# Banded attention stage rewritten: unrolled query blocks, row maximum on 32 queries by 160 keys, stacking transfers from SBUF

## The chip, the cores and the metric

The program runs on one core of one Trainium2 chip. The metric is the device time of one execution in microseconds. The program is four stages in a row (attention, a routed two-level expert layer, a state-space layer, a soft mixture of experts); only the first, attention, is changed, and an all-engine barrier stands behind it.

## The reference

With x of shape 2048 x 128, 16 heads of 8 channels:

```
xn  = layernorm(x)                       # no gain, no offset
q, k, v = split(xn @ Wqkv + bqkv)        # 16 heads of 8
s   = (q . k) * 8**-0.5,  only where |i - j| <= 64, else the lowest float
out = softmax(s) @ v
x   = x + layernorm(out @ Wout + bout)
... three more stages follow, each x = x + layernorm(stage(layernorm(x)))
```

## The kernel before

**Number format.** q and k are split into three bf16 parts each (h, m, l: high, middle, low). A score is one matmul over 48 rows, six products of parts times 8 channels, held in two "stacks": `qs` and `ks`, 128 partitions, where partitions 0 to 63 hold the even heads and 64 to 127 the odd ones (48 rows of parts and, in `ks`, 16 rows of flags that forbid the padding keys). Eight head pairs `j` lie side by side along the free axis.

**Set-up.** x is loaded in one transfer, normalized (`ln_x`), transposed by TensorE, and projected chunk by chunk (512 tokens, L514 to L525). ScalarE and VectorE make the three parts (L464 to L468, L348 to L352). SyncE then writes the parts to DRAM (`parts_scratch`, L274) and reads them back into the stacks, 24 transfers of 8 partitions each per group of tokens (L283; groups of 512, 512 and 1024 tokens). Meanwhile GpSimd fills both stacks with constants (L290, L291).

**Windows.** Queries go in 17 blocks ("windows") of 128, offset by 64, each against 256 keys. VectorE first copies a window of the stacks to `kw` and `qw` (`window`, L358, L359) and of v to `vw` (`window_v`, L362). For each window and each group g of four heads (4 groups):
- `natural(w, g)`: two matmuls of 512 columns with the identity put the band mask (-1e30 outside) into PSUM (L536), four matmuls of 128 queries by 256 keys add the scores (L541). VectorE takes the negated maximum of each query over the 1024 columns (`maxima`, L366). `parts(w)` splits the 16 maxima of each query into three bf16 parts (L375 to L381), TensorE transposes them (`maxima_t`, L581) and VectorE takes them back (`m_t`, L388).
- `transposed(s, g)`: four matmuls of 256 columns with a selection matrix add the maxima (L553), eight matmuls add the scores, keys on the partitions (L559). ScalarE exponentiates 1024 columns at once (`exps`, L474). GpSimd zeroes what lies outside the band with two affine selects (L316, L318).
- `values(s, g)`: eight matmuls in column tiles of 32 multiply by v and a column of ones (L573).
Then `values_nat` transposes (L587), VectorE divides (`norm`, L398, L401), `attn_t` transposes (L592). `project` (L599) runs in the last window for all 16 tiles; bias, `ln_y` and the addition to x follow at the end (L437, L75 to L143).

**Order.** Each engine has its list written out by hand: `body` for one window, run by `steps`: window 0, a hardware loop over 14 windows, two per round, then windows 15 and 16. In one round TensorE does `natural` of window s+1 beside `transposed` of window s; the scores of `natural` have two pairs of PSUM banks, those of `transposed` one pair, so `transposed(g)` waits for the exponential of g-1. Engines are in order, and all waits are semaphores.

## Time and profile before

| | |
|---|---|
| median of 3 runs | 856.33 us (854.08 to 858.31) |
| profiled execution, its own time | 861.29 us |
| its span, first to last instruction | 859.5 us |
| busy share of the span: TensorE, VectorE, ScalarE, GpSimd | 77%, 61%, 40%, 42% |
| mean granted TensorE clock | 0.904 of full |

The profile has a page of the whole execution and a trace that can be asked for groups of instructions, for the busy time in a stretch, for waits, for transfers and for the instructions in order of time. Attention is the stretch from 0 to 291.9 us, where the first transfer of the next stage is issued.

### The profile page before, as it was taken

The page shows a single profiled execution, that of the slowest core. Times are in us where ns is not written, and L with a number is a line of the kernel's source. Part 1 is how long each engine was busy: PE and PEld are TensorE (multiplying, and loading weights), DVE is VectorE, ACT ScalarE, POOL GpSimd, SP SyncE. Part 2 cuts the span into 40 slices and gives each one's busy share as a digit, 9 for nine tenths or more (in the row PEclk, how much of TensorE's full clock was granted, in tenths as well). Part 3 has the DMA queues.
Part 4 walks back from the last instruction along what each step waited for, and adds up shares of the span by engine and source line. Part 5 has one row for each costly group of instructions (what it writes and reads, how often), then busy time and mean ns, then how long its engine had stood idle before and what let it go on. Part 6 is the DMA issues. An engine that isn't in the chain of part 4 may idle for free. (4 is left out here: it accounts for less than half of the span.)

```text
span 859.5 us, 18332 instructions
## 1 busy us (share of the span) xinstructions
PE 660.1 (77%) x7554; PEld 384.0 (45%) x7554; DVE 525.7 (61%) x1094; ACT 344.9 (40%) x522; POOL 359.2 (42%) x330
## 2 busy tenths in 40 slices
PE   0617888888888279976977498058998988999995
PEld 0302444444445179876876234023333344444442
DVE  8647667676664733342413667869999974406266
ACT  1421433444344573242414552346544536434320
POOL 9202444444444300000001253228999974966530
PEclk9967999999999559997977689669999999999998
DMA  3156552000000364000000640000000000000000
GB/s 76 37 107 108 89 72 32 0 0 0 0 0 2 111 199 100 3 4 2 4 4 5 261 112 0 0 1 0 0 1 0 0 1 1 1 0 1 12 13 25
DMA packets 17327, 29.76 MB, mean 35 GB/s; under 512 B 3248, under 2 KB 13168, under 8 KB 16240
## 3 DMA queue, kind: packets, MB, share of 16 engines
q1 hardware_dynamic: 17264, 28.87, 14.1%
q8 instruction: 46, 0.75, 0.4%
q14 instruction: 17, 0.14, 0.1%
HBM read 24.54 MB, written 4.19 MB: 33 GB/s over the span
## 5 line engine op out<-in xcount | busy, mean ns | idle before, releaser
L474 ACT ACTIVATE pr_exp<-at_psum 128x1024 f32<-128x1024 f32 x68 | 69.6, 1023 | 131.9 <-PE at_psum L559 131.9
L366 DVE TENSOR_REDUCE pr_neg_max<-at_psum 128x4 f32<-128x1024 f32 x68 | 83.2, 1225 | 49.8 <-PE at_psum L541 49.8
L316 POOL TENSOR_SCALAR_AFFINE_SELECT pr_exp<-pr_exp 128x512 f32<-128x512 f32 x68 | 47.1, 692 | 159.0 <-ACT pr_exp L474 159.0
L1493 POOL TENSOR_TENSOR all_phi_b<-all_phi_b,mo_work 128x512 f32<-128x512 f32 x56 | 71.1, 1269 | 43.3 <-ACT mo_work L1699 38.6
L749 POOL TENSOR_TENSOR all_x<-all_x,ff_x_blocks 128x512 f32<-128x512 f32 x3 | 3.8, 1263 | 173.0 <-ACT ff_x_blocks L940 173.0
L1514 PE MATMUL all_psum<-all_phi,mo_xt 128*128 128x512 f32 x128 | 67.1, 651 | 7.3 <-ACT mo_work L1681 5.6
L536 PE MATMUL at_psum<-band_mask,all_ident_bf 128*128 128x512 bf16 x136 | 43.1, 400 | 38.3 <-DVE pr_q_window L359 38.3
L1463 POOL TENSOR_TENSOR mo_work<-mo_work,mo_max 128x1024 f32<-128x1024 f32 x32 | 61.3, 1916 | 22.1 <-DVE mo_max L1755 22.1
L1547 PE MATMUL all_psum<-mo_xt,all_phi_centred 128*128 128x512 f32 x128 | 65.4, 591 | 0.0
L1600 PE MATMUL all_psum<-mo_work,mo_y_slots 128*128 128x512 f32 x128 | 62.5, 595 | 1.8 <-DVE mo_work L1803 1.8
L1699 ACT ACTIVATE mo_work<-all_psum 128x512 f32<-128x512 f32 x64 | 37.7, 601 | 60.6 <-PE all_psum L1547 60.6
L1469 POOL TENSOR_TENSOR mo_dispatch<-mo_work,mo_rsum 128x1024 f32<-128x1024 f32 x32 | 61.3, 1917 | 0.0
L1523 PE MATMUL all_psum<-mo_dispatch,mo_xn 128*128 128x512 f32 x128 | 60.2, 595 | 0.0
L1685 ACT ACTIVATE mo_work<-mo_work 128x1024 f32<-128x1024 f32 x32 | 33.9, 1058 | 55.5 <-POOL mo_work L1463 55.5
L1803 DVE TENSOR_TENSOR mo_work<-mo_work,all_psum 128x512 f32<-128x512 f32 x64 | 38.9, 683 | 11.9 <-PE all_psum L1589 11.9
L553 PE MATMUL at_psum<-pr_neg_max_t,band_select 128*128 128x256 bf16 x272 | 41.6, 276 | 5.9 <-ACT pr_exp L474 5.5
L318 POOL TENSOR_SCALAR_AFFINE_SELECT pr_exp<-pr_exp 128x512 f32<-128x512 f32 x68 | 45.8, 674 | 0.0
L1514 PEld LDWEIGHTS all_psum<-all_phi,mo_xt 128*128 128x128 f32 x128 | 23.6, 200 | 46.9 <-ACT mo_work L1681 24.0
L1755 DVE TENSOR_REDUCE mo_max<-mo_work 128x32 f32<-128x1024 f32 x32 | 38.7, 1208 | 7.1 <-ACT mo_work L1681 7.1
L573 PE MATMUL at_psum<-pr_exp,pr_v_window 128*32 128x128 f32 x1088 | 41.7, 278 | 1.4 <-POOL pr_exp L318 1.4
L1762 DVE TENSOR_REDUCE mo_sum<-mo_work 128x32 f32<-128x1024 f32 x32 | 38.7, 1209 | 0.0
L1523 PEld LDWEIGHTS all_psum<-mo_dispatch,mo_xn 128*128 128x128 f32 x128 | 24.5, 192 | 31.0 <-issue 29.9
(339 smaller groups left out, 1340.2 us busy)
## 6 DMA issues: line engine op xcount, KB each, us to landing
all_expert_w<-in_expert_w SPq DMA_DIRECT2D x1, 4096.0 KB, 18.3
ff_b_up<-in_b_up SPq DMA_DIRECT2D x1, 2048.0 KB, 10.2
ff_a_up<-in_a_up SPq DMA_DIRECT2D x1, 2048.0 KB, 16.1
ff_w_down<-in_w_down SPq DMA_DIRECT2D x2, 1024.0 KB, 20.5
at_q_stack<-parts_scratch SPq DMA_DIRECT2D x24, 64.0 KB
at_k_stack<-parts_scratch SPq DMA_DIRECT2D x24, 64.0 KB
at_q_stack<-parts_scratch SPq DMA_DIRECT2D x12, 128.0 KB
at_k_stack<-parts_scratch SPq DMA_DIRECT2D x12, 128.0 KB
```

The lines of the kernel that those rows point to most:

```text
L316: nc.gpsimd.affine_select(out=e[:, g, :, 0, :], in_=e[:, g, :, 0, :], compare_op=ALU.is_ge, fill=0.0, base=0, pattern=[[0, GH], [-1, P]], ...
L318: nc.gpsimd.affine_select(out=e[:, g, :, 1, :], in_=e[:, g, :, 1, :], compare_op=ALU.is_ge, fill=0.0, base=0, pattern=[[0, GH], [1, P]], c ...
L366: nc.vector.tensor_reduce(negm[:, GH * g:GH * g + GH].rearrange("p (u r) -> p r u", r=2), psum[:, SN + 2 * (g % 2):SN + 2 * (g % 2) + 2, : ...
L474: nc.scalar.activation(e[:, g, :, :, :].rearrange("p h j q -> p (h j q)"), psum[:, ST:ST + 2, :].rearrange("p b n -> p (b n)"), ACT.Exp).t ...
L536: nc.tensor.matmul(psum[:, SN + 2 * (g % 2) + r, :], c["identb"][:, :], c["mask"][:, :, :].rearrange("p a b -> p (a b)"), start=True, stop ...
L1463: nc.gpsimd.tensor_tensor(cells(ls[:, u % 4, :]), cells(lc[:, u % 4, :]), to_cells(mn[:, u % 4, :]), ALU.subtract).then_inc(sub_done, 1)
L1469: nc.gpsimd.tensor_tensor(cells(dn[:, u % 4, :]), cells(ls[:, u % 4, :]), to_cells(rs[:, u % 4, :]), ALU.mult).then_inc(d_ready, 1)
L1493: nc.gpsimd.tensor_tensor(tot[:, ch % 2, :], first, ec[:, ch % 2, j, :], ALU.add).then_inc(added, 1)
L1514: last = nc.tensor.matmul(psum[:, 2 * hf + k, :], xt[:, P * z:P * z + P], phi_d[:, HALF * hf + W * k:HALF * hf + W * k + W], start=True, s ...
L1523: last = nc.tensor.matmul(psum[:, 4 + 2 * hf + k, :], xn[:, z, :], dn[:, u % 4, W * k:W * k + W], start=(z == 0), stop=(z == NT - 1))
L1547: nc.tensor.matmul(psum[:, n % 3, :], phi[:, P * j:P * j + P], xt[:, cols], start=False, stop=True).then_inc(cl_done, 1)
L1600: nc.tensor.matmul(psum[:, 5 + ch % 2, :], yt[:, j, :], ec[:, ch % 2, j, :], start=(j == 0), stop=(j == NJ - 1)).then_inc(y_done, 1)
```

## The change

- The stacks are filled straight from the parts in SBUF, without DRAM: the projection's columns are laid out so that 64 contiguous partitions hold one half. There are again 24 transfers of 8 partitions per group, but ordered by part: first all that need h, then m, then l, so that the first can go before the others are computed. The input is loaded in three pieces.
- The padding keys are flagged in one row (48), set up by six transfers `rows_in`; GpSimd fills only the edges of the stacks.
- The negated maximum enters the score matmul itself: its three parts are three more rows (49 to 51) of `qs`, against ones in `ks`. They get there by two small transfers per window (`maxima_in`), for which SyncE waits; the matmuls of `transposed` now take 52 rows and no selection matmul stands before them.
- The maximum is taken over 32 queries by 160 keys (the band of 32 queries is 160 wide): a unit is two heads of one half, eight matmuls of 49 rows, 32 query columns, 160 keys, in four column tiles. No mask matmul: VectorE adds a 128x160 mask and takes the minimum in one instruction, two per unit, 16 per window.
- A unit of `transposed` is two heads too (four matmuls, one PSUM bank), and the exponential is 128x512, eight per window. Both `natural` and `transposed` have rings of three banks. No copies `kw`, `qw`, `vw`: the loop is unrolled and reads the stacks directly.
- `natural` runs two windows ahead. `project` runs one tile per window within the loop, the bias as a matmul with a row of ones; ScalarE takes the result, VectorE its statistics. The residual of tiles 0 to 11 is done in the last two windows.
- TensorE runs 24 matmuls of 512 columns (`keep_warm`) ahead of the first window.

The diff, cut to its core (`+` and `-` lines only, declarations and most waits left out):

```diff
-                            sp.dma_start(scratch["hml".index(k), :, :, r0:r1].rearrange("w p n -> p w n"), kept[:, :, r0:r1]).then_inc(bounced[ch], 16)
-                                    sp.dma_start(stack[p0:p0 + 8, :, pad + r0:pad + r1], rows[half][:, :, r0:r1]).then_inc(stacked[ch], 16)
+                def stack(group, kind):
+                    r0, r1 = STACKS[group]
+                    sp.wait_ge({"h": hi_ready, "m": mid_ready, "l": low_ready}[kind], 2 * r1 // 512)
...
+                                    sp.dma_start(dst[p0:p0 + DH, :, pad + r0:pad + r1], part[k][64 * half:64 * half + 64, which, r0:r1]).then_inc(stacked[group], 16)
+                def maxima_in(w):
+                    sp.wait_ge(mt_ready, w + 1)
+                    for half in range(2):
+                        p0 = 64 * half + PARTS
+                        sp.dma_start(qs[p0:p0 + 3, :, w * P:w * P + P], m_t[24 * half:24 * half + 24, w % 2, :]).then_inc(nm_in[w % 2], 16)
+                for kind in "hml":
+                    stack(0, kind)
+                stack(1, "h")
+                maxima_in(0)
+                stack(1, "m")
+                stack(1, "l")
+                maxima_in(1)
+                for n, kind in enumerate("hml"):
+                    stack(2, kind)
+                    maxima_in(2 + n)
+                for w in range(5, NW):
+                    maxima_in(w)
...
-                    nc.gpsimd.memset(ks[:, :, :].rearrange("p j n -> p (j n)").bitcast(F32), 0.0)
-                    nc.gpsimd.memset(qs[:, :, :].rearrange("p j n -> p (j n)").bitcast(F32), ONE_ONE).then_inc(filled, 2)
+                nc.gpsimd.memset(qs[:, :, 0:64], 0.0)
...
-                        nc.vector.tensor_copy(kw[:, wp, :, :], ks[:, :, bass.ds(w * P, 2 * P)])
-                        nc.vector.tensor_copy(qw[:, wp, :, :], qs[:, :, bass.ds(w * P, P)]).then_inc(win, 1)
-                        nc.vector.tensor_reduce(negm[:, GH * g:GH * g + GH].rearrange("p (u r) -> p r u", r=2),
+                        last = v.tensor_tensor_reduce(out=masked[:, 2 * (k % 3) + i, :], in0=psum[:, SN + n % 3, WIN * i:WIN * i + WIN], in1=mask[:, :], scale=-1.0, scalar=3.0e38,
+                                                      op0=ALU.add, op1=ALU.min, accum_out=nm[:, r, 0, j:j + 1])
...
+                    nc.scalar.activation(e[:, m // 2, 2 * (m % 2):2 * (m % 2) + 2, :, :].rearrange("p h j q -> p (h j q)"), psum[:, ST + n % 3, :], ACT.Exp, scale=scale).then_inc(exp_done, 1)
...
-                            nc.tensor.matmul(psum[:, SN + 2 * (g % 2) + r, :], c["identb"][:, :], c["mask"][:, :, :].rearrange("p a b -> p (a b)"),
+                def natural(w, m):
...
+                    for i in range(2):
+                        r, j = head(m, i)
+                        rows = slice(64 * r, 64 * r + PARTS)
+                        for q in range(0, P, QC):
+                            k0 = w * P + q
+                            last = nc.tensor.matmul(psum[q:q + QC, SN + n % 3, WIN * i:WIN * i + WIN], qs[rows, j, k0:k0 + QC], ks[rows, j, k0:k0 + WIN], start=True, stop=True)
+                def transposed(w, m):
+                    n = NU * w + m
+                    if m == 0:
+                        pe.wait_ge(nm_in[w % 2], 32 * (w // 2 + 1))
+                    if n >= 3:
+                        pe.wait_ge(exp_done, n - 2)
+                    for i in range(2):
+                        r, j = head(m, i)
+                        rows = slice(64 * r, 64 * r + PARTS + 3)
+                        for b in range(2):
+                            last = nc.tensor.matmul(psum[:, ST + n % 3, 256 * i + P * b:256 * i + P * b + P], ks[rows, j, (w + b) * P:(w + b) * P + P], qs[rows, j, w * P:w * P + P], start=True, stop=True)
+                def project(t):
...
+                    nc.tensor.matmul(psum[:, SN + n % 3, 0:P], one[:, :], bias[:, :], start=True, stop=False)
+                    nc.tensor.matmul(psum[:, SN + n % 3, 0:P], a_t[:, col:col + P], wout[:, :], start=False, stop=True).then_inc(sn_done, 1)
...
+                keep_warm(WARM)
...
+                for s in range(NW):
+                    for m in range(NU):
+                        transposed(s, m)
+                        if s + 2 < NW:
+                            natural(s + 2, m)
+                        if m == 0 and s >= 1:
+                            values(s - 1, 2)
+                        if m == 1 and s >= 1 and s + 1 < NW:
+                            maxima_t(s + 1)
+                        if m == 1 and s >= 3:
+                            project(s - 3)
+                        if m == 2 and s >= 1:
+                            values(s - 1, 3)
+                        if m == 4 and s >= 1:
+                            values_nat(s - 1)
+                        if m == 4:
+                            values(s, 0)
+                        if m == 6 and s >= 1:
+                            attn_t(s - 1)
+                        if m == 6:
+                            values(s, 1)
```

VectorE's order in one round is `maxima(s + 2, m)` for m = 0 to 7, the statistics of one projected tile behind m = 1, `norm(s - 1)` behind m = 5, and `parts(s + 2)` at the end. ScalarE's is `exps(s, m)`, with `take_maxima(s + 1)` behind m = 1, the copies of the values and of the projected tile behind m = 2, and that of the attention tile behind m = 6.

## Rows read from the trace of the kernel before

**Rows 1.** Busy time, clock and transfers in four stretches of attention and in two windows.

```profile
core 0: us, PE busy (x) PEld busy (x) DVE busy (x) ACT busy (x) POOL busy (x), PEclk, DMA share, GB/s
15.00:65.00 50.00, 16.30 (x64) 10.45 (x64) 29.86 (x45) 16.09 (x30) 11.77 (x10) 0.84 0.32 65
...
74.00:278.00 204.00, 173.02 (x2409) 93.31 (x2409) 135.44 (x253) 82.05 (x101) 89.70 (x136) 0.99 0.18 29
278.00:292.00 14.00, 3.17 (x13) 2.19 (x11) 8.79 (x34) 4.95 (x11) 3.56 (x9) 0.50 0.00 0
```

**Rows 2.** TensorE's instructions in order of time, one window in the loop.

```profile
157.49 0.60 PE L536 MATMUL at_psum<-band_mask,all_ident_bf 128*128 128x512 bf16 x2 [1.34 <-DVE pr_q_window L359]
158.03 0.39 PE L541 MATMUL at_psum<-pr_k_window,pr_q_window 64*128 64x256 bf16 x4
158.35 0.61 PE L553 MATMUL at_psum<-pr_neg_max_t,band_select 128*128 128x256 bf16 x4
158.90 0.40 PE L559 MATMUL at_psum<-pr_q_window,pr_k_window 64*128 64x128 bf16 x8
159.22 0.66 PE L573 MATMUL at_psum<-pr_exp,pr_v_window 128*32 128x128 f32 x16
159.82 0.61 PE L536 MATMUL at_psum<-band_mask,all_ident_bf 128*128 128x512 bf16 x2
...
166.94 1.12 PE L573 MATMUL at_psum<-pr_exp,pr_v_window 128*32 128x128 f32 x32
...
169.56 0.60 PE L536 MATMUL at_psum<-band_mask,all_ident_bf 128*128 128x512 bf16 x2 [1.34 <-DVE pr_q_window L359]
```

**Rows 3.** Groups by line and shape, one window (157.5 to 169.55 us).

```profile
L366 DVE TENSOR_REDUCE pr_neg_max<-at_psum 128x4 f32<-128x1024 f32 x4 | 4.9, 1225 | 3.0 <-PE at_psum L541 3.0
L474 ACT ACTIVATE pr_exp<-at_psum 128x1024 f32<-128x1024 f32 x4 | 4.1, 1024 | 6.5 <-PE at_psum L559 6.5
...
L553 PE MATMUL at_psum<-pr_neg_max_t,band_select 128*128 128x256 bf16 x16 | 2.4, 274 | 0.3 <-ACT pr_exp L474 0.3
...
L559 PEld LDWEIGHTS at_psum<-pr_q_window,pr_k_window 64*128 64x128 bf16 x32 | 0.9, 94 | 0.8 <-issue 0.8
```

**Rows 4.** Groups by line and shape, attention and the start of the next stage (0 to 340 us).

```profile
L316 POOL TENSOR_SCALAR_AFFINE_SELECT pr_exp<-pr_exp 128x512 f32<-128x512 f32 x68 | 47.1, 692 | 159.0 <-ACT pr_exp L474 159.0
...
L485 ACT COPY pr_values_t<-at_psum 128x512 f32<-128x512 f32 x17 | 9.9, 581 | 2.9 <-PE at_psum L573 2.9
...
L401 DVE TENSOR_TENSOR pr_attn<-at_psum,pr_rec 128x64 f32<-128x64 f32 x34 | 6.0, 219 | 0.6
...
L437 DVE TENSOR_TENSOR pr_xn<-at_psum,at_bout 128x512 f32<-128x512 f32 x4 | 2.7, 679 | 3.0 <-PE at_psum L599 3.0
```

**Rows 5.** All engines in order of time, set-up.

```profile
11.13 8.02 DVE L88 TENSOR_SCALAR pr_ln_x_tmp<-pr_ln_x_tmp 128x16 f32<-128x16 f32 x1
...
43.28 4.13 SPq L283 DMA_DIRECT2D at_q_stack<-parts_scratch  x12
...
64.06 0.69 DVE L358 COPY pr_k_window<-at_k_stack 128x2048 bf16<-128x2048 bf16 x1 [11.73 <-SPq L252]
...
65.24 1.01 PE L536 MATMUL at_psum<-band_mask,all_ident_bf 128*128 128x512 bf16 x2 [18.41 <-DVE pr_q_window L359]
```

**Rows 6.** Transfers from 92 to 140 us, the third stacking group.

```profile
DMA packets 1762, 3.25 MB, mean 68 GB/s; under 512 B 200, under 2 KB 200, under 8 KB 1757
q1 hardware_dynamic: 1757, 3.19, 49.5%
```

**Rows 7.** Busy time and transfers, while parts are written to DRAM.

```profile
39.00:43.00 4.00, 2.85 (x12) 1.73 (x12) 3.87 (x7) 2.04 (x5) 0.00 (x0) 1.00 0.59 197
```

**Rows 8.** All engines in order of time, end of attention.

```profile
280.15 1.28 ACT L112 ACT_TABLE_LOAD   x1
280.18 2.08 PE L599 MATMUL at_psum<-at_wout,at_attn_t 128*128 128x128 f32 x8 [0.35 <-ACT at_attn_t L479]
...
285.67 3.19 ACT L130 ACTIVATE pr_xn<-pr_xn,at_ln_y_tmp 128x128 f32<-128x128 f32 x8 [0.53 <-DVE at_ln_y_tmp L102]
...
291.88 0.36 SPq L727 DMA_DIRECT2D ff_w_up<-in_w_up  x1
```

More of the change, by code:

```diff
@@ L632, in _ @@
[L632 to L643 removed]
+                            last = nc.tensor.matmul(psum[32 * k:32 * k + DH + 1, PV, P * g:P * g + P], v9[:, w + b, h, :], e[:, g, k, b, :], start=(b == 0), stop=(b == 1))
```

830 lines of the change are left out of this document (417 added, 413 removed).

## The prediction

> **What bounds the kernel now.** I read the busy time in stretches first, to see which parts of attention are of one kind [rows 1]. There are four: set-up to 65 us, a short start of the first window, the windows from 74 to 278, and a tail to 291.9, where the next stage's first transfer goes out [rows 8]. Nothing after 291.9 is changed, so the question is where that point moves.
>
> Set-up: the first matmul of the first window starts at 65.24 after TensorE stood 18.4 us; VectorE had waited 11.7 us for SyncE's word that the first group is stacked, and the 24 transfers of that group were issued from 43.28 [rows 5]. So the end of set-up is set by writing the parts out, reading them back (43.3 to about 64), and by how early the parts exist. One part of that is an accident: a tiny VectorE instruction took 8.02 us beside GpSimd's fill of the stacks (L88).
>
> Windows: in time order TensorE has one window from 157.49 to 169.56, 12.07 us [rows 2], of which it is busy about 85% (173.0 of 204) [rows 1]. The groups show the others well below: VectorE 135 of 204, GpSimd 90, ScalarE 82. Of TensorE's idle time 1.34 us stands at the window's head, waiting for the copy of q (L359), behind maxima, parts and copies on VectorE. So the windows are bound by TensorE plus that turn.
>
> Read from the order of time how a group of matmuls is priced [rows 2]. From the first start of one group to that of the next: 2 of 512 columns 0.54 us, 4 of 256 in two row halves 0.32, 4 of 256 on all rows 0.55, 8 of 128 in two halves 0.32, 8 f32 in column tiles (16 records) 0.60. At 2.4 GHz two of 512 stream in 0.43; four of 256 in 0.43 alone or 0.21 where two halves run side by side; eight of 128 in halves 0.21. The difference is 0.11 each time: every group here changes the tile shape, and a change costs 0.11 us. The 32 records of L573 take 1.12 with a single one's latency of about 0.27 in it, so 0.85/31 = 27 ns from start to start in column tiles.
>
> **The change, part by part.**
>
> Set-up. The load in pieces and the missing 8 us at L88 let the first parts exist early: load 4 to 5 us, statistics, scale, four transposes, one copy, projection. In the old trace the same chain without the stall is about 15 us, so the stacking transfers start at about 15 instead of 43.3, and the trip to DRAM is gone. The 24 issues take 8.3 us (12 in 4.13 [rows 5]) and are hidden behind their own data.
>
> Transfers. Bytes are unchanged: 1.57 MB, 1.57 MB, 3.15 MB. The trace has 68 GB/s for the third group [rows 6], with the transfer engines half busy (49.5%), and 1.57 MB in 20.8 us, 76 GB/s, for the first. Both write into 8 partitions per transfer, as the new ones do; only the source differs. I take 74 GB/s. The bounds: 68, and 197 GB/s, the pace where 128 partitions were read out [rows 7]. Group 0 is then stacked at 15 + 2 + 21 = 38. The projection chain on ScalarE and VectorE (about 4 us a chunk, from L485-like copies of 0.58 and splits of 0.68 [rows 4]) ends near 33, and 24 warming matmuls, partly at half clock, take 7 to 8. First `natural` at about 41 against 65.2.
>
> But now the new wait. Each window's maxima travel by `maxima_in`, and in SyncE's list these stand between the stacking groups; what is queued ahead of them on the transfer engines must land first. Queued behind SyncE's waiting are the next stacking transfers; behind the landing are `transposed` of that window and, TensorE being in order, everything. Window 0's maxima (ready about 47) land behind the h-part of group 1, at 50; window 1's behind the rest of group 1, at 61; window 2's behind the h-part of group 2 (1.57 MB, 21 us), at 83; window 3's behind m (1.05 MB, 14 us), at 97; window 4's behind l, at 104. So windows 0 to 3 run at the pace of transfers, 4 of them in 59 us instead of 48, and part of what set-up gained is given back. Window 3 starts at 97, takes 10 and, TensorE having stood idle, perhaps 2 more at half clock: window 4 starts at 109. The old kernel would be there at 74 + 4 x 12.07 = 122.
>
> One window from there on, TensorE. `transposed`: 4 matmuls of 128 columns, all in one half now: 4 x 53 ns + 0.11 = 0.32, eight times 2.6 us. `natural`: 8 matmuls of 160 columns (67 ns) in four column tiles, so 17 ns each by stream, but 27 ns is the closest spacing the trace has for column tiles: 8 x 27 ns + 0.11 = 0.32, eight times 2.6. `values` as now: 4 x 0.60 = 2.4. Transposes of values, maxima and attention 1.0. `project`: two f32 matmuls, 0.5. Together 9.1 us, against 10.2 busy now (173.0/204 of 12.07): the mask (4 x 0.54) and selection (4 x 0.55) matmuls go, 4.4 us, and twice as many groups pay the 0.11 and lose the side-by-side halves.
>
> No instruction here shows the new VectorE operation. Nearest: an addition from PSUM of 64 columns takes 219 ns, of 512 columns 679 ns, which interpolates to 318 for 160 [rows 4]; overlapped with its neighbour 0.25. Lower bound 16 x 0.25 = 4.0 us; upper, if the reduction costs a second pass as dear as the first, 16 x 0.64 = 10.2. I take 0.3, 4.8 us, since the reduce of 1024 columns at 1225 ns [rows 3] runs at the same pace per column as an addition. With parts, norm and statistics (1.6) VectorE is at 6.4. ScalarE: eight exponentials near 0.58 (the 512-column copy [rows 4]) plus four copies: 6.0. GpSimd: 8 x 0.69 = 5.5 [rows 4], hidden under TensorE. All below 9.
>
> One stall: at m = 6 TensorE waits in `attn_t` for `norm`, which VectorE starts only behind `maxima` of m = 5: 0.15 + 0.6 + 0.75 us after that unit, of which TensorE has 0.64 in hand. About 0.6 to 0.9; I take 0.6. The 1.34 us turn is gone, since `natural` runs two windows ahead. Window: 9.1 + 0.6 = 9.7 us, against 12.07. Bounds: 9.1, and by VectorE's upper price 11.8.
>
> What weighs against this on TensorE is weight loads: 96 per window, each for a short matmul. In the trace loads take 94 ns [rows 3] and are hidden: L553 loads full-height weights four times, and its group still takes its streams plus 0.11 [rows 2]. The Trainium skill, "TensorE: Matmul & The Clock Gate", Part 3 (The mechanism), says a weight load overlaps matmuls in flight only when it goes to other rows of the array; by that rule every load of a unit, all in one half, would be exposed. L553 disagrees with the rule, on full rows; no row here has column tiles in one half.
>
> Tail. Windows 15 and 16 have no `natural`, so GpSimd and ScalarE bound them: 7.4 and 7; window 15 also has two function-table switches of 1.28 us each, 2.6 [rows 8]. The tail after the last window is now 16 us; of it the four-tile projection at half clock (2.08), sixteen scalings (3.19 on ScalarE) and the additions behind shrink to one or two tiles [rows 8]: about 12.
>
> **Sum.** 109 + 11 x 9.7 (106.7) + 10 + 7 + 12 = 244.7, against 291.9: 47 us less. The profiled execution took 861.3, so 814; the median of the runs is 5 lower, 856.3 - 47 = 809 us.
>
> **Rivals.**
> - *The transfers run faster from SBUF.* For it: writes out of SBUF reached 197 GB/s [rows 7]. Against: the engines reading into 8 partitions were half busy throughout, and that shape stays. At twice the pace all data are in by 57, windows run one after the other from 50, window 4 starts at 90: 19 less, 790 us. The Trainium skill, "SBUF — State Buffer", Door 1, gives a port about 27 GB/s and 8 partitions two ports, 54 GB/s. By it window 4 would start near 136 and the kernel take 836; the measured 68 to 76 GB/s into the same shape are above it.
> - *VectorE becomes the bound.* The fused masked minimum costs 0.6 rather than 0.3: 16 x 0.6 + 1.9 = 11.5 a window, 1.8 x 11 = 20 more: 829. For it: no row shows the operation; it has a result of its own to write besides 160 columns. It would show as TensorE waiting for VectorE.
> - *Slower: weight loads are exposed.* Place: `natural` and `transposed`. Price: 96 x 94 ns = 9.0 us a window; 11 windows, two thirds less in the last two, and some 10 us in the first four, 115 in all: near 920 us. It decides from where the gain of 47 is used up over 13 windows, 3.6 us each, 38 ns per matmul. Against it: L553 and the column-tiled L573 at 27 ns.
> - *It does little*: transfers hold the windows longer than I think, since `maxima_in` waits in one list with stacking; a pace of 45 GB/s would put window 4 at 155. Nothing in the rows is that low.
>
> **Numbers.** My forecast 0.56 (own range 797 to 822), faster transfers 0.14, VectorE or smaller TensorE costs above mine 0.20 (to 840), exposed loads 0.06, little 0.04. The range 785 to 838 takes in the first three but for their ends. What this kernel can tell from no change is about 0.5%, 4 us: faster 0.91, same 0.03, slower 0.06.
>
> **What will show it.** First `natural` near 41; TensorE standing before windows 1 to 3, released by a transfer into `q_stack`; `stacked` data until about 104; a window of 9.7 us at full clock, with 0.32 us per unit group and a wait on `norm`; VectorE near 6.4 us of it; the next stage at 245. Wrong if the spacing in `natural` is above 40 ns, if one fused minimum is above 0.4, or if the transfers do not run near 74 GB/s.

## The result, and the profile after

The changed kernel takes 878.67 us (median of 4 runs, 873.13 to 879.62), the kernel before beside it 857.32: a ratio of 1.024, 95% interval 1.018 to 1.030. It is slower by 2.4%, where the prediction had 809 us and faster. (Where a ratio below is not the quotient of the two medians, it leaves out runs more than 1.5% above the fastest of the same kernel.)

The first view is the busy time in stretches of the changed kernel; its columns are those of [rows 1].

```profile
36.00:41.00 5.00, 5.00 (x32) 2.13 (x37) 0.58 (x2) 0.00 (x0) 0.00 (x0) 1.00 0.55 108
41.00:43.00 2.00, 1.02 (x40) 0.41 (x40) 1.55 (x13) 0.00 (x0) 0.00 (x0) 1.00 0.50 103
43.00:44.00 1.00, 0.71 (x16) 0.24 (x16) 1.00 (x10) 0.00 (x0) 0.00 (x0) 0.83 0.54 100
44.00:45.00 1.00, 0.45 (x8) 0.14 (x8) 1.00 (x9) 0.00 (x0) 0.00 (x0) 0.50 0.24 41
45.00:100.00 55.00, 39.27 (x530) 19.48 (x530) 20.87 (x143) 17.97 (x33) 13.43 (x22) 0.50 0.50 71
100.00:120.00 20.00, 19.68 (x230) 10.35 (x232) 8.15 (x52) 7.82 (x16) 7.33 (x12) 0.50 0.06 12
156.50:171.28 14.78, 14.46 (x170) 7.56 (x171) 5.84 (x39) 5.96 (x12) 4.88 (x9) 0.50 0.01 4
```

The column before the transfer share is the granted clock: 1.00 (2.4 GHz) behind `keep_warm`, down to 0.50 (1.2 GHz) within the first window's `natural`, at about 44 us, and 0.50 in every stretch after that. In [rows 1] the windows ran at 0.99. TensorE is busy 14.46 of 14.78 us, a larger share than before, and the slower clock stays. All other engines have time to spare.

TensorE in order of time, the window of the last row, from one transposition of the attention tile (L640) to the next; [rows 2] is the same view before:

```profile
156.50 0.48 PE L640 MATMUL at_psum<-all_ident,at_attn 128*128 128x128 f32 x1 [0.33 <-DVE at_attn L388]
156.91 1.04 PE L620 MATMUL at_psum<-at_exp,at_v_and_one 128*9 128x128 f32 x16
157.88 0.61 PE L610 MATMUL at_psum<-at_q_stack,at_k_stack 52*128 52x128 bf16 x4
158.42 0.46 PE L597 MATMUL at_psum<-at_k_stack,at_q_stack 49*32 49x160 bf16 x8
158.81 0.60 PE L610 MATMUL at_psum<-at_q_stack,at_k_stack 52*128 52x128 bf16 x4
...
162.57 0.80 PE L648 MATMUL at_psum<-at_wout,at_attn_t 128*128 128x128 f32 x2
...
171.28 0.48 PE L640 MATMUL at_psum<-all_ident,at_attn 128*128 128x128 f32 x1 [0.32 <-DVE at_attn L388]
```

From start to start: a unit of `transposed` (L610) 0.54 us, of `natural` (L597) 0.39, of `values` (L620) 0.97. The first is the prediction's own price with the clock halved: 4 x 0.107 + 0.11 = 0.54. The wait for `norm` is there, 0.33 us.

Groups by line and shape, the same window:

```profile
L505 ACT ACTIVATE at_exp<-at_psum 128x512 f32<-128x512 f32 x8 | 4.8, 600 | 7.4 <-PE at_psum L610 7.4
L367 DVE CUSTOM_DVE_ANT_0 at_masked<-at_psum,at_mask 128x160 bf16<-128x160 f32 x17 | 4.6, 320 | 5.7 <-PE at_psum L597 4.2 <-PE at_psum L629 1.5
...
L610 PEld LDWEIGHTS at_psum<-at_q_stack,at_k_stack 52*128 52x128 bf16 x32 | 2.7, 126 | 2.7 <-issue 2.7
...
L367 DVE DVE_READ_ACCUMULATOR2_ANT at_neg_max<- 128x1 f32 x16 | 1.3, 84 | 0.0
```

The new VectorE operation takes 320 ns and a read of its accumulator 84; the loads of weights (126 ns) lie beneath the matmuls. Then the start of three windows, each a `transposed` in TensorE's order of time, and the first transfer of the next stage, which [rows 8] has at 291.88:

```profile
62.61 0.60 PE L610 MATMUL at_psum<-at_q_stack,at_k_stack 52*128 52x128 bf16 x4 [1.76 <-DMA at_q_stack<-at_neg_max_t]
...
86.34 0.60 PE L610 MATMUL at_psum<-at_q_stack,at_k_stack 52*128 52x128 bf16 x4 [10.33 <-DMA at_q_stack<-at_neg_max_t]
...
114.46 0.60 PE L610 MATMUL at_psum<-at_q_stack,at_k_stack 52*128 52x128 bf16 x4
...
277.04 0.60 PE L610 MATMUL at_psum<-at_q_stack,at_k_stack 52*128 52x128 bf16 x4
...
312.68 0.37 SPq L787 DMA_DIRECT2D ff_w_up<-in_w_up  x1
```

Windows 1, 2, 4 and 15 start there. Window 4 is 5.5 us later than foreseen (109). Eleven windows take 162.6, 14.78 each and not 9.7: 56 us. From window 15 to the next stage it is 35.6 and not 29: 6.6. Together 68, the distance from 244.7 to 312.7. So five sixths of the error is the length of a window. That the clock makes this length is shown below, by the same units at full clock (e10). The question for the experiments is why the clock is at its lower level.

### The profile page after: what moved, and what is told of

Same layout as the page of the kernel before. It is cut to its first block and busy times, and to the rows that moved or that the text cites. A ratio compares the mean times of both kernels' runs of the same rounds, so it can differ in the third digit from the quotient of the medians.

```text
span 877.7 us, 19514 instructions
## 1 busy us (share of the span) xinstructions
PE 722.5 (82%) x8020; PEld 415.3 (47%) x8020; DVE 466.4 (53%) x1491; ACT 365.9 (42%) x626; POOL 334.1 (38%) x331
## 5 line engine op out<-in xcount | busy, mean ns | idle before, releaser
L505 ACT ACTIVATE at_exp<-at_psum 128x512 f32<-128x512 f32 x136 | 80.7, 600 | 124.2 <-PE at_psum L610 124.2
L367 DVE CUSTOM_DVE_ANT_0 at_masked<-at_psum,at_mask 128x160 bf16<-128x160 f32 x272 | 72.8, 320 | 107.3 <-PE at_psum L597 73.8
L319 POOL TENSOR_SCALAR_AFFINE_SELECT at_exp<-at_exp 128x512 f32<-128x512 f32 x68 | 45.4, 668 | 206.1 <-ACT at_exp L505 206.1
L610 PE MATMUL at_psum<-at_q_stack,at_k_stack 52*128 52x128 bf16 x544 | 79.2, 303 | 12.1 <-DMA at_q_stack<-at_neg_max_t 12.1
L620 PE MATMUL at_psum<-at_exp,at_v_and_one 128*9 128x128 f32 x1088 | 70.9, 409 | 2.5 <-POOL at_exp L321 2.3
L610 PEld LDWEIGHTS at_psum<-at_q_stack,at_k_stack 52*128 52x128 bf16 x544 | 44.6, 126 | 55.4 <-issue 39.6
L597 PE MATMUL at_psum<-at_k_stack,at_q_stack 49*32 49x160 bf16 x1088 | 59.9, 320 | 2.0 <-DVE at_neg_max L367 1.7
L620 PEld LDWEIGHTS at_psum<-at_exp,at_v_and_one 128*9 128x9 f32 x1088 | 30.1, 116 | 27.9 <-issue 13.7
L321 POOL TENSOR_SCALAR_AFFINE_SELECT at_exp<-at_exp 128x512 f32<-128x512 f32 x68 | 43.1, 634 | 0.0
```

What stands on the lines that cost most here:

```text
L367: last = v.tensor_tensor_reduce(out=masked[:, 2 * (k % 3) + i, :], in0=psum[:, SN + n % 3, WIN * i:WIN * i + WIN], in1=mask[:, :], scale=- ...
L505: nc.scalar.activation(e[:, m // 2, 2 * (m % 2):2 * (m % 2) + 2, :, :].rearrange("p h j q -> p (h j q)"), psum[:, ST + n % 3, :], ACT.Exp, ...
L597: last = nc.tensor.matmul(psum[q:q + QC, SN + n % 3, WIN * i:WIN * i + WIN], qs[rows, j, k0:k0 + QC], ks[rows, j, k0:k0 + WIN], start=True ...
L610: last = nc.tensor.matmul(psum[:, ST + n % 3, 256 * i + P * b:256 * i + P * b + P], ks[rows, j, (w + b) * P:(w + b) * P + P], qs[rows, j, ...
L620: last = nc.tensor.matmul(psum[32 * k:32 * k + DH + 1, PV, P * g:P * g + P], v9[:, w + b, h, :], e[:, g, k, b, :], start=(b == 0), stop=(b ...
```

## The experiments

Of each kernel the granted clock is given for 100 to 220 us of its profiled execution; before has 1.00 there and after 0.50. Diffs are against the changed kernel, or, for names with b, against the kernel before. A "filler" is one 128x128 by 512-column bf16 matmul into a bank that the next group overwrites. Five kernels were timed in one run only ("one run" below); their times are single executions beside the median of before on the same chip.

**Filling TensorE.** e1_fill_each adds a filler ahead of every unit of `transposed`, e4_fill_half ahead of every second.

```diff
+                    nc.tensor.matmul(psum[:, ST + n % 3, 0:512].rearrange("p (k n) -> p k n", k=4), c["identb"][:, :], c["identb"][:, :].unsqueeze(1).broadcast_to([P, 4, P]), start=True, stop=True)
```

> The changed kernel with one more matmul in each unit of transposed: the identity, 128 rows by 128 columns, against 512 columns, into the bank that the unit's own matmuls then overwrite. Eight per window, nothing else changed. Theory A (the clock stays at its lower level because the windows' matmuls fill only 49 to 52 rows and column tiles of 32, and the work, not its history, decides): the granted clock goes to 1.00 in the windows, a window takes my predicted 9.7 us plus 8 x (0.21 + 0.11) = 12.3 instead of 14.78, and the kernel takes about 878 - 13 x 2.5 = 846 us. Rival B (the clock fell in the first window's short bursts and the transfer waits and can't come back in any such loop; the work doesn't matter): it stays at 0.50, a window takes 14.78 + 8 x (0.43 + 0.11) = 19.1, the kernel about 934 us.

> As the kernel with a filler of 128 rows by 128 columns against 512 columns, but only in every second unit of transposed, four per window. Theory A (the kind of work decides the clock): if half the filler is enough, clock 1.00, a window of 9.7 + 4 x 0.32 = 11.0 us, the kernel about 878 - 13 x 3.8 = 829 us; if not, clock 0.50 and 14.78 + 4 x 0.54 = 16.9, about 906 us. Rival B (only history decides): 0.50 and about 906 us.

Measured: 930.73 us, ratio 1.089 (1.079 to 1.099), and 908.59, 1.059 (1.053 to 1.064). In both TensorE is busy without a gap, and the clock is 0.50: the expectation for a clock that stays down held within 4 us. The busy time of e1, columns as above:

```profile
100.00:180.00 80.00, 80.00 (x776) 35.81 (x779) 27.12 (x169) 26.19 (x52) 21.99 (x36) 0.50 0.01 3
```

Too little work, or gaps between bursts, is not what keeps the changed kernel's clock down.

**The shape of `natural`.** e2_wide makes it 128 queries by 256 keys, without column tiles; e6_qc64 makes it two tiles of 64 by 192; `consts` is waited for at 4 and 6.

```diff
-    QC, WIN = 32, 160
+    QC, WIN = 128, 256
```

> The changed kernel with natural's tile back at 128 queries by 256 keys: two matmuls of 256 columns per unit on all 128 columns of the array, 49 rows as before, no column tiles; mask and fused minimum are 256 wide. Theory A in the form that the column tiles alone hold the clock down: clock 1.00, a unit of natural 0.32 us, a window near 10 us. Theory A in the form that the rows count as well (49 to 52 of 128 here and in transposed): clock stays 0.50, a unit of natural takes 2 x 0.213 + 0.11 = 0.54 against 0.385, a window 14.78 + 8 x 0.15 = 16.0 us, the kernel near 895 us. VectorE's minimum goes from 320 to about 420 ns, 6.7 us a window, no bound in either.

> The changed kernel with natural on 64 queries by 192 keys: four matmuls a unit in two column tiles of 64. Number of changes of tile shape as in the changed kernel. Theory C: more of the array is filled than with 32, less than with 128: the granted clock lies between 0.50 and the 0.60 of the wide kernel. Rival D (changes of shape decide): 0.50 exactly, as in the changed kernel. At 0.50 a unit of natural is 4 x 0.160 / 2 + 0.11 = 0.43 us, a window 15.1, about 883 us.

Measured: e2_wide 866.83 us (one run), clock 0.56, changing between 0.50 and 0.80 in stretches of 20 us; e6_qc64 883.23 (one run), clock 0.50. Without tiles in `natural` the clock is still down most of the time; that the tiles have a part in it rests on this one run. TensorE in order of time in e2:

```profile
155.98 0.41 PE L610 MATMUL at_psum<-at_q_stack,at_k_stack 52*128 52x128 bf16 x6
156.22 0.27 PE L597 MATMUL at_psum<-at_k_stack,at_q_stack 49*128 49x256 bf16 x1
156.24 0.27 PE L610 MATMUL at_psum<-at_q_stack,at_k_stack 52*128 52x128 bf16 x2
```

A unit of `transposed` has four matmuls, and in the program two of `natural` stand behind them. Here six of `transposed` start before the first of `natural`: the next unit, which lies in the other row half, has begun beside the one in front of it. So TensorE, which the kernel's description calls in order, is not strictly so between the two halves. With `natural` in the same tile shape as `transposed`, two halves run side by side although no pair is issued alternately; in the changed kernel, where `natural` has column tiles, they never do (each unit there takes its full streams).

**Row halves side by side.** e3_side issues the units of `transposed` in pairs, one in each half of the rows, matmul by matmul.

```diff
+                    for i in range(2):
+                        for b in range(2):
+                            for u in range(2):
+                                r, j = head(m + u, i)
+                                rows = slice(64 * r, 64 * r + PARTS + 3)
+                                last[u] = nc.tensor.matmul(psum[:, ST + (n + u) % 3, 256 * i + P * b:256 * i + P * b + P], ks[rows, j, (w + b) * P:(w + b) * P + P], qs[rows, j, w * P:w * P + P], start=True, stop=True)
...
-                        transposed(s, m)
+                        if m % 2 == 0:
+                            transposed_pair(s, m)
```

> The changed kernel with two units of transposed issued as one, its eight matmuls alternating between the two row halves (each half keeps its own PSUM bank), so that two can stream side by side as in the kernel before. natural is left as it is. At half clock eight matmuls of 128 columns side by side take 4 x 0.107 + 0.11 = 0.54 us instead of 1.07: a window 14.78 - 4 x 0.53 = 12.7 us, the kernel about 878 - 15 x 2.1 = 846 us, if the clock stays at 0.50. If rows in use decide and both halves together (104 of 128) are enough, the clock is 1.00 and a window near 9.0 us: about 805 us. If the loads of weights were the price, and not the streams, alternating halves would save at either clock more than 0.53 a pair.

Measured: 850.97 us, 0.990 (0.981 to 0.998). The clock is still 0.50. A pair takes 0.54 us, what one unit took, so a window loses 4 x 0.54:

```profile
151.12 0.61 PE L625 MATMUL at_psum<-at_q_stack,at_k_stack 52*128 52x128 bf16 x8
151.66 0.46 PE L597 MATMUL at_psum<-at_k_stack,at_q_stack 49*32 49x160 bf16 x8
```

e5_wide_side is e2 with both kinds in pairs (the diff of e3, and that of e11 below):

> The changed kernel with both: natural on 128 queries by 256 keys without column tiles, and the units of natural and of transposed issued in pairs, the matmuls alternating between the row halves. No matmul of the scores is then in a column tile, and both halves stream side by side; only values stays in column tiles. Theory C (a filler of full matmuls did not bring the clock back, the missing column tiles did in part: what keeps it low is the share of work in column tiles and in one half, and enough of the opposite turns it): clock well above the 0.60 of the wide kernel, towards 1.00; VectorE, 16 x (0.42 + 0.08) + 1.9 = 9.9 us, is then the bound, about 812 us. Rival D (the clock goes with the number of changes of tile shape, not with the tiles): here natural and transposed share one shape, so D too expects it to rise. If the clock stays at 0.50: 4 pairs of 0.43 + 0.43, values 3.9, transposes and projection 3.3, a window of 10.9 us, about 825 us.

Measured: 830.12 us, 0.965 (0.962 to 0.969), clock 0.72; TensorE now stands for VectorE (L367). Its TensorE is busy for 94.50 of the 120 us, that of e2 for 107.28, and its clock is the higher one: against e2 only the order of the same matmuls has changed.

**The values' columns.** `v9` (eight channels and a one) widened to 32 columns in e7_pad32, and to 30 in e8_wide_side_pad on top of e5; the matmul of `values` takes as many.

```diff
-        v9 = a.sb("v_and_one", [P, NT + 2, H, DH + 1])
+        v9 = a.sb("v_and_one", [P, NT + 2, H, 32])
```

> The changed kernel with v widened to 32 columns per head (the other columns hold ones and go unused), so that a matmul of values fills its column tile of 32 as in the kernel before, instead of 9 columns of it. Rival F in this form (9 of 32 columns is what the clock misses): clock rises above 0.50, a window towards 9.7 us. Theory C: clock 0.50 and 878 us as before the edit, since natural is untouched and a load of 32 columns is no dearer than one of 9 (116 ns each with 9).

> The kernel with wide natural and both halves side by side, and v widened to 30 columns per head. If the share of the array in columns matters, values at 30 of 32 columns lifts the clock from 0.73 to 0.79 towards 1.00, and VectorE's waits stay: 815 to 822 us. If it does not: 830 us as without.

Measured: 889.25 us (one run), clock 0.50; and 838.21, 0.977 (0.972 to 0.982), clock 0.74. Widening the nine columns does not raise the clock by itself; e8's 0.74 is no gain that could be told from e5's 0.72.

**Fillers on e5.** e9_wide_side_fill adds one per pair, four per window.

> The kernel with wide natural and both halves side by side, and one filler matmul (identity, 128 by 128, 512 columns) per pair of units, four per window. With the column tiles of natural in place eight such fillers left the clock at 0.50. Theory C: without them four are enough for 1.00, since the kernel before without its mask matmuls held 1.00 with the like of four such fillers per window. The fillers cost 4 x 0.32 = 1.3 us of TensorE, which at full clock has 8.0 + 1.3 = 9.3 us of work and VectorE 9.9: about 815 us. If the clock stays near 0.76, the fillers are pure cost: about 840 us.

Measured: 822.62 us, 0.955 (0.952 to 0.958), clock 0.90, and 1.00 from 120 to 160 us. A filler that did nothing for the clock in e1 raises it here; e12 below has it with the column tiles too. (The expectation counts b1's selection matmuls, sixteen of 256 columns a window, as four fillers; they are the like of eight.)

**The kernel before, with one thing taken away.** b1_no_mask leaves out the band mask's matmuls (the maximum is over all 256 keys); b2_no_sel leaves out the selection matmuls (the maximum is not subtracted); b3_tiles computes `natural` in tiles of 32 queries by 160 keys on top of the unchanged mask; b4_one_half issues the score matmuls of one half and then those of the other.

```diff
-                        for r in range(2):
-                            nc.tensor.matmul(psum[:, SN + 2 * (g % 2) + r, :], c["identb"][:, :], c["mask"][:, :, :].rearrange("p a b -> p (a b)"),
...
-                        for r in range(2):
-                            for u in range(2):
-                                nc.tensor.matmul(psum[:, ST + r, 256 * u:256 * u + 256].rearrange("p (j q) -> p j q", j=2), c["sel"][:, 4 * g + 2 * u + r, :],
...
+                                for q in range(0, P, 32):
+                                    last = nc.tensor.matmul(psum[q:q + 32, SN + 2 * (g % 2) + r, 256 * u + q:256 * u + q + 160], qw[rows, wp, 2 * g + u, q:q + 32],
+                                                            kw[rows, wp, 2 * g + u, q:q + 160], start=False, stop=(u == 1))
...
-                        for u in range(2):
-                            for r in range(2):
+                        for r in range(2):
+                            for u in range(2):
```

(b1, b2, b3 and b4 in this order.)

> The kernel before without the mask matmuls of natural (the maximum is then taken over all 256 keys, which a softmax does not mind). Eight full matmuls of 512 columns less per window. Theory C: full-array work goes from the mix, the clock falls from 1.00 in part or whole; at 0.50 in the whole loop a window would be about 2 x 7.9 + 1.3 = 16 us and the kernel about 910 us. Rival E (in the kernel before the clock is up for another reason, and these matmuls are only cost): clock 1.00, a window 12.07 - 4 x 0.54 = 9.9 us or what VectorE's turn leaves of it, 10.4, and the kernel about 830 us.

> The kernel before without the selection matmuls of transposed: the maxima are computed but not subtracted before the exponential. Sixteen full matmuls of 256 columns less per window. Theory C: the clock falls in part or whole, the kernel is slower or gains much less than the work it leaves out; whole loop at 0.50: about 910 us. Rival E: clock 1.00, a window 12.07 - 4 x 0.55 = 9.9 to 10.4 us, the kernel about 830 us.

> The kernel before with one part of the change alone: the scores of natural come in column tiles, 32 queries by 160 keys, sixteen matmuls per group of four heads instead of four of 128 by 256, alternating between the row halves as before, added onto the unchanged mask. Theory C (column tiles in natural are what takes the clock down): clock 0.50 in the loop, a window of about 2 x 10.8 + 1.3 = 23 us, the kernel near 1000 us; partly down, in between. Rival F (column tiles by themselves do no harm; transposed on one half, or values with 9 instead of 32 columns, does): clock stays 1.00, a group of natural takes 16 x 0.027 + 0.11 = 0.54 instead of 0.32, a window 12.9, the kernel about 872 us.

> The kernel before with the matmuls of natural and transposed in another order: all of one row half, then all of the other, instead of alternating, so that two no longer stream side by side. Same matmuls. Theory G (what the clock misses in the changed kernel is the second half at work beside the first): clock below 1.00 in the loop, towards 0.50, the kernel far above 900 us. Rival H (order of halves is only time, the clock does not mind): clock 1.00, a group of natural 0.54 instead of 0.32 and of transposed 0.54 instead of 0.33, a window of 12.07 + 4 x 0.43 = 13.8, the kernel about 889 us.

Measured: b1 849.3 us, 0.987 (0.983 to 0.991), clock 1.00; b2 838.52, 0.977 (0.972 to 0.983), clock 0.96; b3 859.83, 0.999 (0.997 to 1.001), clock 1.00; b4 861.49 (one run, against 856.02), clock 1.00. Without the mask, with tiles in `natural` or with another order of issue the old kernel's clock stays at 1.00, and without the selection it is 0.96: none of the four alone brings it near 0.50. (b1 and b2 also leave TensorE idle for longer: it is busy for 86.59 and 90.09 of the 120 us, before for 101.07.)

b4 did not do what it was made for. Both its theories took groups of 0.54 us, and rival H 889 us. In order of time the groups of score matmuls take about 0.33 us, as before:

```profile
155.50 0.41 PE L559 MATMUL at_psum<-pr_q_window,pr_k_window 64*128 64x128 bf16 x8
155.84 1.12 PE L573 MATMUL at_psum<-pr_exp,pr_v_window 128*32 128x128 f32 x32
...
159.00 0.40 PE L541 MATMUL at_psum<-pr_k_window,pr_q_window 64*128 64x256 bf16 x4
159.33 0.61 PE L553 MATMUL at_psum<-pr_neg_max_t,band_select 128*128 128x256 bf16 x4
```

Eight matmuls of 128 columns one after the other would take 8 x 53 ns + 0.11 = 0.54 us. So the two halves still ran side by side, as in e2. b4 shows that the order of issue does not matter there; what the old kernel's clock does with one half at a time, no run shows.

b3 also measures the spacing of column tiles:

```profile
156.46 0.33 PE L542 MATMUL at_psum<-pr_k_window,pr_q_window 64*32 64x160 bf16 x16
156.72 0.61 PE L554 MATMUL at_psum<-pr_neg_max_t,band_select 128*128 128x256 bf16 x4
```

16 tiled matmuls, from both halves, take 0.26 us to the start of the next group, at most 16 ns each, under the 27 ns that the prediction took.

**A burst in the changed kernel.** e10_burst adds 32 matmuls of 512 columns ahead of window 6.

```diff
+                    if w == 6 and m == 0:
+                        for _ in range(32):
+                            nc.tensor.matmul(psum[:, ST + n % 3, :].rearrange("p (k n) -> p k n", k=4), c["identb"][:, :], c["identb"][:, :].unsqueeze(1).broadcast_to([P, 4, P]), start=True, stop=True)
```

> The changed kernel with one burst of 32 full matmuls of 512 columns (identity) ahead of window 6, 7 to 14 us of TensorE, nothing else. Theory H (history: the changed loop would hold the full clock if it once had it, but can't raise it by itself): the clock rises in the burst and stays at 1.00 to the end of the loop, windows of 9.7 us from there, 11 windows x 5 us less, about 835 us. Theory K (the mix of the changed loop itself does not hold it): the clock rises in the burst and is back at 0.50 within a window, the kernel 878 + 10 = 888 us.

Measured: 884.6 us (one run). TensorE in order of time in e10:

```profile
145.40 8.21 PE L608 MATMUL at_psum<-all_ident_bf 128*128 128x512 bf16 x32
153.54 0.39 PE L613 MATMUL at_psum<-at_q_stack,at_k_stack 52*128 52x128 bf16 x4
...
157.95 0.60 PE L613 MATMUL at_psum<-at_q_stack,at_k_stack 52*128 52x128 bf16 x4
```

And its busy time in stretches:

```profile
145.00:147.00 2.00, 2.00 (x13) 0.71 (x13) 1.42 (x6) 0.60 (x1) 1.22 (x2) 0.50 0.00 0
...
148.00:154.00 6.00, 6.00 (x38) 2.68 (x36) 0.00 (x0) 0.03 (x1) 0.00 (x0) 1.00 0.01 3
154.00:158.00 4.00, 4.00 (x82) 2.43 (x75) 1.06 (x8) 2.39 (x6) 1.22 (x2) 1.00 0.01 2
158.00:159.00 1.00, 1.00 (x17) 0.55 (x14) 0.68 (x4) 1.00 (x4) 0.17 (x1) 0.50 0.02 3
```

The full matmuls raise the clock to 1.00. Behind them the changed kernel's own units run at full clock, 0.33 us for four, and TensorE is not idle for an instant; yet the clock falls at 158 and stays. So the kernel did not merely start badly: its mix does not hold the clock, even without a gap. (One run, but the two levels are read within it.)

**Halves side by side, tiles kept.** e11_side_tiles is e3 with `natural` in pairs too; e12_side_tiles_fill has one filler per pair besides.

```diff
+                        for q in range(0, P, QC):
+                            for u in range(2):
+                                n = nat_unit(w, m + u)
+                                r, j = head(m + u, i)
+                                rows = slice(64 * r, 64 * r + PARTS)
+                                k0 = w * P + q
+                                last = nc.tensor.matmul(psum[q:q + QC, SN + n % 3, WIN * i:WIN * i + WIN], qs[rows, j, k0:k0 + QC], ks[rows, j, k0:k0 + WIN], start=True, stop=True)
...
-                        if s + 2 < NW:
-                            natural(s + 2, m)
+                        if s + 2 < NW and m % 2 == 0:
+                            natural_pair(s + 2, m)
```

> The changed kernel with the units of natural and of transposed both issued in pairs that alternate between the row halves; natural keeps its column tiles of 32 by 160 keys. In the kernel before with the same tiles sixteen such matmuls took 0.26 us to 0.40 us, so a pair of natural should take 0.40 at half clock against 0.77, a window 14.78 - 2.1 - 1.5 = 11.2 us at 0.50, about 832 us. Theory G (halves side by side raise the clock even with tiles): clock above 0.50 and a window towards 7.5 us, about 790 us.

> The kernel with both halves side by side and column tiles, and one filler matmul (identity, 128 by 128, 512 columns) per pair of units, four per window. Four of these lifted the wide kernel from about 0.76 to 0.95. Theory G: here too the clock is up, 0.9 to 1.00, and since VectorE works on 160 columns again (6.4 us a window) nothing else bounds: TensorE 7.5 + 1.3, a window of 8.8 to 9.3 us, about 805 us. If column tiles in natural keep it at 0.50 whatever else there is: 11.2 + 4 x 0.54 = 13.4 us, about 860 us.

Measured: e11 814.33 us (804.67 to 819.9), 0.943 (0.937 to 0.949), clock 0.73; e12 816.4, 0.952 (0.946 to 0.958), clock 0.96. Both beat both kernels, and the four fillers that raise the clock cost about what they bring. The clocks are those of one execution each, and e11's wanders, between 0.67 and 0.84 in stretches of 20 us. In order of time e12 has a window in 9.02 us, from 150.46 (L683) to 159.48, and this is its busy time, all at full clock:

```profile
150.46:159.48 9.02, 7.75 (x176) 4.39 (x175) 6.16 (x38) 5.47 (x12) 4.86 (x8) 1.00 0.02 4
```

TensorE in order of time within it; L626 is now a pair of units of `transposed`, L645 one of `natural`:

```profile
152.10 0.62 PE L656 MATMUL at_psum<-at_exp,at_v_and_one 128*9 128x128 f32 x16
...
152.98 0.40 PE L626 MATMUL at_psum<-at_q_stack,at_k_stack 52*128 52x128 bf16 x8
154.49 0.33 PE L645 MATMUL at_psum<-at_k_stack,at_q_stack 49*32 49x160 bf16 x16 [1.12 <-DVE at_neg_max L367]
154.75 0.66 PE L671 MATMUL at_psum<-all_ident,at_values_t 128*128 128x128 f32 x4
```

**Both kinds of full-height matmul out of the kernel before.** b5_neither is b1 and b2 together; b6_neither_half has b4's order of halves as well.

> The kernel before, without its mask matmuls and without its selection matmuls (the maximum is over all 256 keys and is not subtracted); the score matmuls still alternate between the two row halves. Theory: what keeps the clock up is that both row halves of the array are at work, so halves that alternate are enough: clock near 1.00 in the windows, window bound by VectorE near 11.5, about 835 us. Rival: the clock is kept up by the full-height matmuls of 512 and 256 columns (mask and selection), and one kind of the two is enough, as the runs with one taken out showed; with neither, the clock in the windows falls to about 0.50 although the halves alternate, and the window comes out at 12 us or more, 845 us or more.

> The same, with the score matmuls of one row half first and then those of the other. Theory: without full-height matmuls and without alternating halves the old kernel is in the place of the changed one: clock near 0.50 in the windows from 100 to 260 us, groups at double price, about 865 us. Rival: neither matters in the old kernel and the cause is in the smaller units of the changed one: clock near 1.00, within 1% of the run in which the halves alternate.

Measured: 824.82 us, 0.960 (0.954 to 0.966), and 822.55, 0.958 (0.954 to 0.962). The busy time of b5 from 100 to 220 us:

```profile
100.00:220.00 120.00, 84.56 (x1380) 51.92 (x1374) 101.65 (x177) 56.90 (x70) 63.12 (x94) 0.83 0.10 17
```

Of b6:

```profile
100.00:220.00 120.00, 83.44 (x1365) 52.42 (x1367) 100.31 (x177) 55.71 (x69) 61.07 (x93) 0.83 0.15 22
```

And of the changed kernel:

```profile
100.00:220.00 120.00, 117.42 (x1389) 61.38 (x1388) 48.14 (x310) 48.25 (x97) 40.31 (x66) 0.50 0.02 4
```

Without either kind the old kernel's clock falls to 0.83: neither my theory (1.00 with alternating halves) nor its rival (0.50) holds in full. b6 is no more a run with one half at a time than b4 was: at half clock its eight matmuls from 160.81 to 161.35 take 0.54 us, which is four streams and not eight. Taking both kinds of full-height matmul out went with the fall to 0.83; whether by their size or by the time they filled is not separated, since TensorE is idle for 30% of b5, waiting for VectorE and ScalarE. 70% busy with 0.83 against 98% busy with 0.50 shows once more that busy time alone does not rank these kernels.

## Why the prediction was wrong

By its own steps:

- **Set-up**: first `natural` at 40.93, predicted 41. Right.
- **Transfers and their waits**: TensorE stood 1.76 us before window 1 and 10.33 before window 2, each released by a transfer into `q_stack`; windows started at 51.5, 62.6 and 86.3 (predicted 50, 61, 83), at 70 to 83 GB/s (74 taken). Right, two or three us late. Before window 3 (99.7, predicted 97) no wait was left, since window 2 took 13.3 us at half clock.
- **The failed step** is "One window from there on, TensorE", with its "Window: 9.1 + 0.6 = 9.7 us". Every group was priced at full clock, because [rows 1] shows 0.99; but that was the clock of the *old* mix. I took out 4 x 0.54 of mask and 4 x 0.55 of selection matmuls, all full-height, replaced pairs of halves by units in one half, and never asked whether the clock would stay. No rival had it either: the slower one was exposed weight loads, so that the chance given to "slower" stood on another mechanism. At half clock the window is 14.78, 56 us over 11 windows. That this is the term is shown by the same units at full clock: 0.33 us for four matmuls in e10, and in e12 (paired, with fillers) a window of 9.02 us and the next stage at 244.20, where the prediction had 244.7 for the changed kernel. That agreement is partly luck: pairing saves about what the fillers and a new wait for VectorE (1.12 us) cost. An estimate for the unpaired window at full clock, from the group times of e10 and e12, is 8 x 0.33 + 8 x 0.24 + 4 x 0.56 + 1.86 for transposes and projection + 0.33 of wait = 9.0 us: the clock costs about 5.8 us a window, and my other terms were together 0.7 too dear.
- **Column tiles at 27 ns**: in the changed kernel the stream at half clock hides it: 8 tiled matmuls take 0.39 from start to start, about 35 ns each with the 0.11 off. e10 has them at full clock, 0.24 us for eight with the change of shape in it, so 0.32 was too much by 0.08. The 27 ns of L573 was no limit of column tiles: it was the stream of its own f32 matmuls, and in the changed kernel it doubles with the clock, from (0.56 - 0.11)/16 = 28 ns in e10 to (0.97 - 0.11)/16 = 54. Harmless.
- **VectorE**: fused minimum 0.320 us (0.30 taken), its accumulator read 84 ns partly under the next one; VectorE 5.84 a window (6.4), ScalarE 5.96 (6.0), GpSimd 4.88 (5.5). Right, never the bound. The wait for `norm` was 0.33 (0.6). (The rival's 16 x 0.6 + 1.9 has 1.9 where the window's own sum has 1.6; with that it is 11.2 and not 11.5.)
- **Exposed weight loads**: not there. A unit of four in one row half takes its streams plus 0.11, with loads of 126 ns beneath. The rule that I had weighed (the Trainium skill, "TensorE: Matmul & The Clock Gate", Part 3, The mechanism: a load overlaps only when it goes to other rows) would have exposed them; by that reading a unit would take 4 x (107 + 126) ns and more, 0.93 us and not 0.54, so the traces disagree with it. The same section of the Trainium skill also lets a load go ahead into a background weight buffer, and with that the traces agree.
- **Tail**: 35.6 us from window 15 on, 29 predicted; its matmuls too are at 0.50 (how much of the 6.6 that makes was not measured), and GpSimd's select took 2.93 us once, at 296.50, against 0.63 otherwise, beside the residual's additions on VectorE (L437).

**What sets the clock, as far as it is shown.** In the changed kernel it is not too little work (e1, e4) and not a bad start (e10), and widening the values' nine columns does not raise it (e7). In the old one neither the mask's nor the selection's absence alone (b1, b2), nor column tiles alone (b3), take it near 0.50. One pattern goes through all the runs. Where at most one kind of score matmul had its two row halves at work side by side, the clock was 0.50: the changed kernel, e1, e3, e4, e6, e7, and e10 but for its burst. Where both kinds had, it was above: 0.56 in e2 (where only units with nothing else between them meet), 0.72 to 0.74 in e5, e8 and e11, 0.83 in b5 and b6, 0.90 to 1.00 in e9, e12, b1 to b4 and the kernel before. e11 is the clean step of this: against e3 it pairs `natural` as well, and the clock goes from 0.50 to 0.73. Full matmuls then raise it further (0.96 in e12), but without it they did nothing (e1).

That this is the cause is not shown. Pairing also halves the number of groups and so of changes of tile shape; but the old kernel has some 20 groups in a window of 12.07 us at 1.00, so these changes alone do not decide. The score matmuls use 49 and 52 rows of a half in the changed kernel and 64 in the old, and no run varies that. What orders the runs above 0.50, between 0.56 and 1.00, is open.

The share of the array's cells at work, taken as an average, does not order them. An estimate from the records of 100 to 220 us (rows by columns of each matmul, times the columns it streams, over what 128 by 128 cells pass at the granted clock, each f32 record counted once): 0.37 in e1 and 0.32 in e7, both at a clock of 0.50, against 0.29 in e12 at 0.96, and 0.24 in the changed kernel as in e11, at 0.50 and 0.73. The Trainium skill, "TensorE: Matmul & The Clock Gate", Part 1 (What's actually happening), ties the clock to how busy the engine has recently been; by it a stream that is 98% busy should run at 2.4 GHz, and here the trace has 1.2.

## What to carry to other kernels

A granted clock read from the old trace belongs to the old mix of matmuls. When a change takes out large full-height matmuls and puts small ones on part of the array in their place, or breaks up pairs that ran in the two row halves side by side, price the stretch at both levels and give the lower one a chance, even where TensorE is never idle; the stretch view of the new kernel answers it in one row. If the clock is down, first see that both row halves run side by side, in every kind of small matmul: where groups of other tile shapes stand between, issue the two halves' matmuls alternately. Here that was worth 7 to 8% of the whole kernel (878.67 to 814.33 us; 1.024 to 0.943 of the kernel before), by saving streams and by raising the clock. Read from the group's time whether the halves really overlap, and not from the order in the program. That b4 and b6 were to run one half at a time and did not is seen only there.

## What the runs showed of the hardware

- TensorE busy 80.00 of 80 us, eight fillers of 512 columns a window among them, stays at a granted clock of 0.50 (e1).
- After 32 full matmuls the clock was 1.00, and it fell again, at 158 us, in a gapless stream of the kernel's own small ones (e10).
- Matmuls of the two row halves ran side by side without being issued alternately, where they had one tile shape: a group of eight of 128 columns took 0.34 us and not 0.54 (b4), and in e2 six matmuls of `transposed` started before the first of the `natural` in front of two of them.
- Column tiles of 32x160 with halves alternating start at most 16 ns apart on average (b3, 0.26 us for 16).
- VectorE's fused add, minimum and reduce over 128x160 from PSUM takes 320 ns, plus 84 ns for the accumulator.
